# The table that sorts tokens to experts: eight tiles in one VectorE comparison, products by GpSimd

## The reference

```
probs = softmax(x @ gate_w.T); w, idx = top_k(probs, 2); w = w / sum(w)
for each expert e:  acc += combine[:, e] * (silu(x @ g_e.T) * (x @ u_e.T)) @ down_e.T
x = x + 0.5 * acc
```

## Time and profile before

| | us |
|---|---|
| three runs, lowest, median, highest | 3594.05, 3595.54, 3597.10 |
| the profiled execution, its own time | 3594.57 |
| its span, first to last instruction | 3592.1 |
| TensorE busy | 3056.1 (85%) |
| VectorE busy | 2473.6 (69%) |
| ScalarE busy | 2050.5 (57%) |
| GpSimd busy | 1225.9 (34%) |

### The profile page before, as it was taken

One profiled execution on the slowest core, in us unless ns is written; L12 is line 12 of the kernel. 1 busy time (PEld: TensorE's weight loads), 2 busy tenths in 40 slices (PEclk: granted clock), 3 DMA queues, 4 the chain that ended last, 5 costly groups with the idle time before them and its releaser, 6 DMA issues. The chain is left out here.

```text
span 3592.1 us, 61777 instructions
## 1 busy us (share of the span) xinstructions
PE 3056.1 (85%) x20359; PEld 1916.5 (53%) x20359; DVE 2473.6 (69%) x6861; ACT 2050.5 (57%) x3077; POOL 1225.9 (34%) x1324
## 2 busy tenths in 40 slices
PE   4759999877567967999999869789868986998999
PEld 2533333344346863222222358658756875887787
DVE  8878998576875448999999454464586445656565
ACT  1238999764233545999999735433343334563564
POOL 3454551021447642001000166566636660001000
PEclk8879999988787987999999979889989998999999
DMA  1033441000021123001000231221202122000100
GB/s 58 1 116 123 136 128 43 2 1 1 24 85 63 48 76 106 21 21 30 20 21 12 84 113 48 81 102 47 68 25 90 47 68 88 1 1 3 65 10 12
DMA packets 87166, 187.16 MB, mean 52 GB/s; under 512 B 23168, under 2 KB 41408, under 8 KB 83792
## 3 DMA queue, kind: packets, MB, share of 16 engines
q1 hardware_dynamic: 60048, 117.66, 9.8%
q0 software_dynamic: 26816, 65.58, 6.0%
HBM read 121.23 MB, written 61.34 MB: 51 GB/s over the span
## 5 line engine op out<-in xcount | busy, mean ns | idle before, releaser
L2579 ACT ACTIVATE core_pr<-core_two 128x1024 f32<-128x1024 f32 (+3 forms) x896 | 787.5, 934 | 49.8 <-PE core_two L2546 46.0
L2615 DVE TENSOR_REDUCE core_mx<-core_one 128x1 f32<-128x512 f32 x778 | 491.4, 684 | 20.8 <-PE core_one L2498 13.6
L2558 PE MATMUL core_ps_o<-core_pr,core_vals 128*32 128x512 f32 (+3 forms) x3584 | 434.1, 559 | 1.8 <-ACT core_oT L2590 1.5
L2498 PE MATMUL core_one<-arena,queries 64*128 64x512 bf16 (+3 forms) x1472 | 375.8, 364 | 27.8 <-PEq L62 17.9
L2546 PE MATMUL core_two<-queries,arena 64*128 64x512 bf16 (+3 forms) x1792 | 341.6, 360 | 8.9 <-ACT core_pr L2579 6.6
L2498 PEld LDWEIGHTS core_one<-arena,queries 64*128 64x128 bf16 x1472 | 113.3, 94 | 295.9 <-DVE core_mx L2615 131.9
L2432 POOL COPY core_vals<-arena 128x288 f32<-128x288 f32 x32 | 14.7, 460 | 691.6 <-PE core_ps_o L2558 691.6
L2609 DVE CUSTOM_DVE_ANT_0 core_junk<-core_one,core_over 128x512 bf16<-128x512 f32 (+4 forms) x334 | 201.9, 644 | 26.3 <-PE core_one L2498 21.9
L2546 PEld LDWEIGHTS core_two<-queries,arena 64*128 64x128 bf16 x1792 | 94.2, 94 | 201.2 <-ACT core_pr L2579 145.2
L2585 ACT ACTIVATE core_over<-core_two 128x1024 f32<-128x1024 f32 (+4 forms) x167 | 159.9, 958 | 58.5 <-PE core_two L2521 45.7
L110 DVE CAST moe_second_x_hi<-moe_second_bank 128x128 fp32r<-128x128 f32 x142 | 41.4, 291 | 215.9 <-PE moe_second_bank L565 215.8
(11 more groups left out here) (655 smaller groups left out, 7984.5 us busy)
## 6 DMA issues: line engine op xcount, KB each, us to landing
arena<-expert_out SPq DMA_DIRECT2D x64, 256.0 KB, 3.8
expert_rows<-arena SPq DMA_DIRECT2D x13, 512.0 KB, 8.3
core_w_raw<-in_m_up POOLq DMA_DIRECT2D x25, 256.0 KB, 3.3
m_hi<-core_w_hi POOLq DMA_DIRECT2D x25, 256.0 KB, 2.4
m_lo<-core_w_lo POOLq DMA_DIRECT2D x25, 256.0 KB, 3.0
q_parts<-qkv_parts SPq DMA_DIRECT2D x16, 384.0 KB, 2.6
k_parts<-qkv_parts SPq DMA_DIRECT2D x16, 384.0 KB, 3.4
queries<-q_parts SPq DMA_DIRECT2D x64, 96.0 KB
```

Source lines behind the costliest of these rows:

```text
L2498: pe.matmul(one[bank[e]][:, 0:width], q_sb[rows, hq, pair, qt * P:(qt + 1) * P], k_sb[rows, hq, pair, kc * CW:kc * CW + width], start=True ...
L2558: mm = pe.matmul(ps_o[h * 32:(h + 1) * 32, off:CW], vals[:, hq % 2, j, h, :], pr[:, (n * N2 + k) % KEPT, h // 2, h % 2, off:CW], start=(j ...
L2579: a.activation(pr[:, step % KEPT, i, :, off:CW], two[spot[e] % 2][:, :, off:CW], ACT.Exp, scale=HD ** -0.5).then_inc(s_wide, 1)
L2615: v.tensor_reduce(at, scores, AX.X, ALU.max).then_inc(s_read, 1)
```

## The change

VectorE now makes all lanes of a group in one comparison of 128 x 8 x 128, with the lane numbers broadcast over the columns and `lo` broadcast over the lanes. It also makes a new tile `hits` (0 or 1, 128 x 8 x 71, bfloat16, two buffers) in one comparison. GpSimd no longer makes lanes: it waits for `hits` and multiplies it by the running number (a row of the float32 slot table, broadcast) into the first half of `cells`. The second half is `hits` times the token's number, on VectorE. From the third group on VectorE also waits until GpSimd has read the `hits` buffer.

```diff
+    hits = st.sb("hits", [P, 2, GT, SLOTS], BF16)
-    OTHERS = (1, 3, 5, 7)
@@ gpsimd
             for n in range(GROUPS_T * TOPK):
                 if n >= 2:
                     p.wait_ge(s_table, n - 1)
-                for k in OTHERS:
-                    j = n * GT + k
-                    last = p.tensor_scalar(lanes[:, n % 2, k, :], r.laneb[:], lo[:, j:j + 1], None, ALU.is_equal)
-                last.then_inc(s_aside, 1)
+                p.wait_ge(s_first, n + 1)
+                p.tensor_tensor(cells[:, n % 2, :, 0:SLOTS], hits[:, n % 2], r.slot[:, n * GT + 1:(n + 1) * GT + 1].unsqueeze(2)
+                                .to_broadcast([P, GT, SLOTS]), ALU.mult).then_inc(s_aside, 1)
@@ vector
             for n in range(GROUPS_T * TOPK):
                 if n >= 2:
                     v.wait_ge(s_table, n - 1)
-                for k in range(GT):
-                    j = n * GT + k
-                    if k not in OTHERS:
-                        v.tensor_scalar(lanes[:, n % 2, k, :], r.laneb[:], lo[:, j:j + 1], None, ALU.is_equal)
-                    last = v.tensor_scalar(cells[:, n % 2, k, 0:SLOTS], r.slotb[:], hi[:, j:j + 1], float(j + 1), ALU.is_equal, ALU.mult)
-                last.then_inc(s_first, 1)
+                at = slice(n * GT, (n + 1) * GT)
+                if n >= 2:
+                    v.wait_ge(s_aside, n - 1)
+                v.tensor_tensor(hits[:, n % 2], r.slotb[:].unsqueeze(1).to_broadcast([P, GT, SLOTS]),
+                                hi[:, at].unsqueeze(2).to_broadcast([P, GT, SLOTS]), ALU.is_equal).then_inc(s_first, 1)
+                v.tensor_tensor(lanes[:, n % 2], r.laneb[:].unsqueeze(1).to_broadcast([P, GT, P]),
+                                lo[:, at].unsqueeze(2).to_broadcast([P, GT, P]), ALU.is_equal)
                 v.wait_ge(s_first, n + 1)
-                v.tensor_scalar(cells[:, n % 2, :, SLOTS:2 * SLOTS], cells[:, n % 2, :, 0:SLOTS], 0.0, r.token, ALU.is_gt, ALU.mult).then_inc(s_cells, 1)
+                v.tensor_scalar(cells[:, n % 2, :, SLOTS:2 * SLOTS], hits[:, n % 2], r.token, None, ALU.mult).then_inc(s_cells, 1)
```

## The result

The changed kernel takes 3610.51 us (median of 7 runs, 3602.53 to 3613.85) against 3597.10 (7 runs) of the kernel before on the same chip: a ratio of 1.0038, 95% interval 1.0026 to 1.0049. It is slower by 13.4 us. The profiled execution has a span of 3608.9 us and a granted clock of 0.927.

What follows compares the result with a forecast made beforehand. The tables were taken to be paced by GpSimd in moe1, with nothing hiding them. Full exclusion added +15.3 (moe1) and +12.9 (moe2), +28.2 on 3594.57, 3622.8; the median lies 1.0 higher: 3624 us, range 3600 to 3645.

Steps and rivals of the forecast that it cites:

- What bounds the kernel, and that nothing hides a table: Four table stretches: GpSimd sets moe1's pace, 2.63 us a group; gathers need the table, so its gain or loss is the kernel's.
- VectorE's new work: Per table group: hits 0.67, lanes 1.22, token product 0.29, together 2.18 us alone, 0.35 to 0.45 under now.
- the two rivals: Tables: port held only at GpSimd's start and end, 3595, chance 0.11; or engines side by side, 3586, chance 0.11.
- the sum: Table period under full exclusion: M + 1.92 = 3.59 us a group; together +28.2 us.
- Exclusion, and its mechanism: Tables: VectorE's two-SBUF-input comparisons and GpSimd's long product go one at a time; chance 0.75, slower, 3609 to 3645.
- The third, strided reads: Tables: broadcast reads slow VectorE by 1.05 us a group, +29 on top of the forecast, 3653; chance 0.03.
- M: Time of GpSimd's new product of 568 columns in each table group: taken as 1.67 us, upper bound 2.25.
- lower bound: GpSimd's product at 1.15 us, from float32 products with a broadcast operand: period 3.07 us, +14, 3609.
- The period but for M: Table group less GpSimd's product: 0.67 + 1.22 - 0.15 - 0.11 + 0.29 = 1.92 us.
- Groups 0 and 1: moe2 tables: would end at 2376.7, still before TensorE's second product at 2378.14, so they cost nothing.
- Groups 2 to 7: moe2 tables: 22.3 us against 15.9 and 15.8 now, +12.9 us for both stages.
- TensorE's clock: moe2, granted 0.97 now: a fall from more idling would slow the first slots, put at 0, bounded by 5 us.

Runs made afterwards that it cites:

- e12_before: The kernel before, unaltered, traced a second time: 3693.32 us in one run, against a median of 3703.77 for it in the same session.
- e2_psum: Changed kernel with slot and lane numbers copied once a stage to PSUM, so each comparison has one SBUF input: ratio 0.9975 to the kernel before.
- e1_alone: Changed kernel with VectorE waiting for GpSimd's product before lanes, so nothing runs beside anything: 3725.69 us against 3698.37 of the kernel before.
- e8_token_first: Changed kernel with the token product put ahead of lanes on VectorE: 3615.13 us against 3599.10 of the kernel before.
- e9_probe2: As e1_alone, with three more GpSimd operations of 568 columns a group to unread tiles: 3858.46 us against 3696.47 of the kernel before.
- e5_small: Kernel before with all eight lanes comparisons of a group on VectorE, GpSimd idle in the table: 3608.16 us against 3599.10 of the kernel before.
- e6_act: As e2_psum, with the token product made by ScalarE instead of VectorE: ratio 0.9960 to the kernel before.

## Why the prediction was right or wrong

**What bounds the kernel, and that nothing hides a table: right.** The tables of the changed kernel are 9.0 us longer in the first pair of traces, 11.0 in the second (110.4 against 99.4). The ratios give 9.4 to 17.6 us and 8.9 to 18.9. So the tables hold the greater part of the loss and perhaps all of it. The remaining 4 us (13.4 less 9.0, and 15.0 less 11.0) are inside both intervals and under the scatter of single traces outside the tables. Whether the change costs something there stays open (e12_before).

**VectorE's new work: right.** 0.74 and 1.21 us against 0.75 and 1.22 forecast. The token product, alone, 0.36. But 2.18 us a group for VectorE alone was too long: it takes lanes at its recorded 1.22 where 1.14 pass to the next start, and e2_psum measured 2.10. That touches the two rivals, not the sum.

**Exclusion, and its mechanism: right.** Both expected marks are in the profile: a GpSimd product that waits inside its own duration for lanes, and a token product that waits for GpSimd. e1_alone and e2_psum tell it from slow forms, e8_token_first shows that the order doesn't matter to the sum but for one wait. The two rivals without full exclusion are out (2.2 to 2.5 us a group; measured 2.95). The third, strided reads, is out by the durations.

**M was mis-sized, and this is the step that failed.** I took 1.67 us for GpSimd's product, "the type is nearer to it than the operation". It takes 1.138 us alone, at my lower bound of 1.15, which came from the rows of the same operation in float32. The 2.43 ns a column belong to the tensor-scalar form, as e9_probe2 shows. 28 groups of 0.53 us too many are 14.9 us, more than half of the 28.2 us forecast. The sum with the lower bound, +14 and 3609, stood in the prediction (its formula gives +3.6 and +3.3 for the two moe1 stages, not +3.7 each, so 13.5 in all), and the result is 3610.5. That the two agree so well is partly luck: the tables themselves grew by 9.0 and 11.0 us, and the rest of the 13.4 stands outside them, where the forecast had nothing and no cause is shown.

**The period but for M: 0.11 us too long.** The formula gives 1.92 + 1.14 = 3.06, measured 2.95. The next hits starts 0.08 us behind GpSimd's end (1095.03 and 1094.95), not 0.18. The token product takes 0.36 us alone and ends 0.16 behind GpSimd, so 0.20 us of it lie beside GpSimd's end, where the row of L1552 had given 0.11.

**moe2.** Groups 0 and 1 cost nothing, as forecast: the first addition still waited for TensorE (it sat idle 3.33 us before 2384.97). Groups 2 to 7 grew by 2.5 and 2.6 us, against 6.4 forecast with M = 1.67 and 3.3 with 1.15. Over the whole stretch moe2_second grew by 1.2 us in the first pair of traces and 2.8 in the second, by the scatter of its first addition. TensorE's clock did not fall there: 0.96 in moe2_first after 0.97, and in moe2_second 0.98 after the 0.93 of this window of the kernel before:

```profile
2725.50:2753.80 28.30, 25.86 (x179) 19.86 (x179) 21.52 (x108) 8.14 (x14) 20.81 (x33) 0.93 0.00 1
```

Range and side were right, and the size of the gap was half the forecast.

## What to carry to other kernels

Before work is shared between VectorE and GpSimd, count the SBUF inputs: a tensor-tensor operation of VectorE with two of them, or a fast one with one (here the token product, 568 columns in 0.36 us), runs in turn with a long GpSimd operation, and the two durations add up. One operand moved to PSUM, where VectorE's price hardly changes, lets both run. For a missing price, the nearest row was here the one with the same operation, not the one with the same type; and an operation whose duration is constant but above its known price can hold a wait inside it, as two did here.

## What the runs showed of the hardware beside that

- On GpSimd, 568 columns take 1.63 us as tensor by constant, 1.14 us as tensor by broadcast tensor and 0.66 us as copy, all with bfloat16 (e9_probe2). In float32 tensor by constant takes the same 1.63 us, and the rows give 1.15 us for the product; the copy has no float32 run at this size.
- A comparison on VectorE that reads one operand from PSUM takes 1.208 us for 1024 columns, against 1.225 alone from SBUF and 1.211 in the changed kernel (e2_psum, and lanes in e1_alone).
- GpSimd's short comparison in the kernel before let VectorE through beside it, and of the 0.64 us of help a group 0.27 was left, where GpSimd's own pace allowed 0.51 (e5_small). What it holds the port for in its 0.6 us was not measured.
- ScalarE's product of 568 columns beside both engines took 0.77 us and disturbed neither (e6_act).
